# A prologue of attention: Wo's weights rounded earlier on ScalarE, five remainders made on GpSimd, and the first q lowered ahead of the first k

## The reference: what is computed

```
qkv = x @ Wqkv;  q, k, v = split(qkv)
q = rope(rmsnorm(q, q_norm_w));  k = rope(rmsnorm(k, k_norm_w))
mask = (i >= j) & (i - j <= 255)
probs = softmax(where(mask, q k^T / sqrt(32), -inf))
x = layernorm(x + (probs v) @ Wo)
shared = (silu(x @ Wg) * (x @ Wu)) @ Ws_down * sigmoid(x @ W_sgate)
x = layernorm(x + shared + sum over 2 experts of combine * expert(x))
```

## Time and profile before

| | |
|---|---|
| median of 3 runs | 1039.35 us (1038.63 to 1040.78) |
| the profiled execution | 1040.8 us, its span 1039.0 us |
| PE busy | 1016.2 us (98%) |
| DVE busy | 768.3 us (74%) |
| ACT busy | 639.3 us (62%) |
| POOL busy | 444.5 us (43%) |
| mean granted clock of TensorE | 0.996 of full speed |

### The profile page before, as it was taken

One profiled execution on the slowest core, in us unless ns is written; L12 is line 12 of the kernel. 1 busy time (PEld: TensorE's weight loads), 2 busy tenths in 40 slices (PEclk: granted clock), 3 DMA queues, 4 the chain that ended last, 5 costly groups with the idle time before them and its releaser, 6 DMA issues.

```text
span 1039.0 us, 19736 instructions
## 1 busy us (share of the span) xinstructions
PE 1016.2 (98%) x7088; PEld 838.1 (81%) x7088; DVE 768.3 (74%) x1163; ACT 639.3 (62%) x1310; POOL 444.5 (43%) x537
## 2 busy tenths in 40 slices
PE   7999999999999999999999999999999999999996
PEld 4677777777777777788888888888888888888884
DVE  6888877888888886596766777676677777667465
ACT  4666666666666765333766666666666666766344
POOL 2688888778888852000122222222222222221163
PEclk9999999999999999999999999999999999999999
DMA  5101111111111024735899999999999999999563
GB/s 194 55 23 44 33 33 33 37 51 34 33 44 33 22 84 147 238 91 167 248 260 264 262 272 266 268 264 256 258 281 259 263 266 271 256 249 255 130 209 146
DMA packets 120981, 171.36 MB, mean 165 GB/s; under 512 B 10114, under 2 KB 63746, under 8 KB 120804
## 3 DMA queue, kind: packets, MB, share of 16 engines
q1 hardware_dynamic: 111856, 149.54, 45.2%
q0 software_dynamic: 8736, 20.45, 11.9%
q10 hardware_dynamic: 292, 0.10, 0.0%
HBM read 151.45 MB, written 23.07 MB: 168 GB/s over the span
## 4 chain that ended last, share of the span: by engine, by line
PE 62%; DVE 1%; DMA 1%; ACT 1%; POOL 1%; issue 0%; SPq 0%; POOLq 0%; ACTq 0%; DVEq 0%
PE gate_ps L1614 4%; PE gate_ps L1616 4%; PE gate_ps L1615 4%; PE up_ps L1614 4%; PE up_ps L1616 4%; PE down_ps L1649 3%; PE up_ps L1615 3%; PE down_ps L1651 3%; PE down_ps L1650 3%; PE e_up_ps L1690 3%; PE e_up_ps L1692 3%; PE e_up_ps L1691 3%; PE e_gate_ps L1699 2%; PE e_gate_ps L1701 2%; PE e_gate_ps L1700 2%; PE e_up_ps L1701 2%
## 5 line engine op out<-in xcount | busy, mean ns | idle before, releaser
L1045 POOL DMA_INDIRECT sum_dram<-rows,target_i x39 | 67.0, 1718 | 358.1 <-ACT rows L1156 358.1
L1449 DVE TENSOR_TENSOR e_lo<-e_raw,e_hi 128x1408 fp32r<-128x1408 f32 x78 | 126.8, 1625 | 47.9 <-ACT e_hi L1130 47.8
L1130 ACT CAST e_hi<-e_raw 128x1408 fp32r<-128x1408 f32 x78 | 107.5, 1378 | 50.4 <-PE e_up_ps L1701 49.9
L337 ACT ACTIVATE prob<-score_ps,nbias 128x256 f32<-128x256 f32 (+1 forms) x256 | 118.2, 471 | 5.0 <-DVE nbias L466 5.0
L272 POOL TENSOR_TENSOR probT<-probT,masks 128x256 f32<-128x256 f32 x128 | 91.8, 745 | 55.4 <-DVE probT L496 55.4
L1454 DVE TENSOR_TENSOR ed_lo<-ed_raw,ed_hi 128x1024 fp32r<-128x1024 f32 x39 | 47.8, 1226 | 64.0 <-ACT ed_hi L1138 63.9
L466 DVE TENSOR_REDUCE nbias<-score_ps 128x2 f32<-128x512 f32 (+1 forms) x128 | 86.3, 675 | 4.4
L1051 POOL DMA_INDIRECT rows<-x_dram,token_i x39 | 50.2, 1287 | 88.7 <-DVE target_i L1416 65.1
L344 ACT COPY probT<-probT_ps 128x512 f32<-128x512 f32 x64 | 37.6, 587 | 78.9 <-PE probT_ps L612 78.8
L579 PE MATMUL proj_ps<-wqkv_lo,xT_hi 128*128 128x512 f32 x180 | 78.0, 434 | 1.2 <-ACT squares L358 1.2
L1614 PE MATMUL gate_ps<-x_hi,gu_lo 128*128 128x512 f32 x180 | 72.3, 402 | 0.6 <-DVE gu_lo L1304 0.6
(11 more groups left out here) (283 smaller groups left out, 2973.5 us busy)
## 6 DMA issues: line engine op xcount, KB each, us to landing
e_raw<-in_We_gu SPq DMA_DIRECT2D x78, 704.0 KB, 6.3
ed_raw<-in_We_down SPq DMA_DIRECT2D x39, 512.0 KB, 5.4
raw_ring<-in_Ws_gu SPq DMA_DIRECT2D x58, 256.0 KB, 6.4
wd_raw<-in_Ws_down SPq DMA_DIRECT2D x44, 256.0 KB, 6.5
gu_raw<-in_Ws_gu SPq DMA_DIRECT2D x30, 256.0 KB, 6.2
ed_raw<-in_We_down SPq DMA_DIRECT2D x39, 192.0 KB, 6.8
xT_in<-in_xT SPq DMA_DIRECT2D x16, 256.0 KB, 2.7
x_in<-in_x SPq DMA_DIRECT2D x16, 256.0 KB, 3.1
```

The costliest lines, as they stand in the source:

```text
L337: nc.scalar.activation(prob[:, g % 2, h, seen], score_ps[:, h, seen], ACT.Exp, bias=nbias[:, s % 2, head:head + 1], scale=1.0, accum_out=r ...
L1130: nc.scalar.copy(e_hi[:, half * HK:(half + 1) * HK, :], raw_half(i, half)).then_inc(e_hi_made, 1)
L1449: nc.vector.tensor_tensor(e_lo[:, part, :], raw_half(i, half), e_hi[:, part, :].bitcast(FP32), ALU.subtract).then_inc(e_lo_made, 1)
```

## The change

Three things change, all of them in the first 45 us.

- ScalarE rounds all four pieces of Wo one after the other in the prologue, behind `split_xT(1)` and ahead of `take_k(0)`, and no longer one in each group of block 0.
- GpSimd, behind the norms of the first q and k, makes the remainders of the values' second half (rows 2 and 3, 128x1024) and then those of Wo's four pieces (128x512 each); VectorE makes neither any more. They count on `cleared` (6, then 7 to 10), and TensorE waits for that.
- VectorE lowers the first q ahead of the first k.

```diff
--- before.py
+++ after.py
@@ -286,8 +286,16 @@
                     for keys in (kT_hi, kT_lo):
                         nc.gpsimd.tensor_copy(keys[:, :, a % RING, :], keys[:, :, key_slot(a % RING), :]).then_inc(kT_copied, 1)
 
+            def split_wo(k):
+                pool.wait_ge(w_hi_made, 6 + k + 1)
+                nc.gpsimd.tensor_tensor(wo_lo[:, k, :], wo_raw[:, k, :], wo_hi[:, k, :].bitcast(FP32), ALU.subtract).then_inc(cleared, 1)
+
             rms_of(0, 0, q_sq, q_var, q_rms)
             rms_of(0, 1, k_sq, k_var, k_rms)
+            pool.wait_ge(w_hi_made, 6)
+            nc.gpsimd.tensor_tensor(wqkv_lo[:, 2, 2:4, :], wqkv_raw[:, 2, 2:4, :], wqkv_hi[:, 2, 2:4, :].bitcast(FP32), ALU.subtract).then_inc(cleared, 1)
+            for k in range(KT):
+                split_wo(k)
 
             for s, g in steps():
                 a, n = s + 1, 4 * s + g - 1
@@ -398,13 +406,13 @@
             first_trig(1, k_rms, k_cs)
             take_q(0)
             split_xT(1)
+            for k in range(KT):
+                split_wo(k)
             take_k(0)
             take_v(0)
 
             for s, g in steps():
                 a, n = s + 1, 4 * s + g - 1
-                if s == 0:
-                    split_wo(g)
                 if g == 2 and has(s - 1):
                     wait(act, oT_made, s)
                     nc.scalar.copy(oT_hi[:, :, :], tiled(oT[:, :])).then_inc(oT_hi_made, 1)
@@ -445,10 +453,6 @@
                 dve.wait_ge(w_hi_made, 2 * c + i + 1)
                 nc.vector.tensor_tensor(wqkv_lo[part], wqkv_raw[part], wqkv_hi[part].bitcast(FP32), ALU.subtract).then_inc(w_lo_made, 1)
 
-            def split_wo(k):
-                dve.wait_ge(w_hi_made, 6 + k + 1)
-                nc.vector.tensor_tensor(wo_lo[:, k, :], wo_raw[:, k, :], wo_hi[:, k, :].bitcast(FP32), ALU.subtract).then_inc(w_lo_made, 1)
-
             def masked_max(s, g, pair):
 
                 done = 2 * (4 * s + g) + pair + 1
@@ -511,9 +515,8 @@
             dve.wait_ge(q_rot, 1)
             rotate_cos(dve, nc.vector, 0, 1, res[:, :], k_cs, k_weighted, k_part)
             rotate_sin(dve, nc.vector, 0, 1, res[:, :], oT[:, :], k_part, k_rot)
-            split_wqkv(2, 1)
+            lower_q(0)
             lower_k(0)
-            lower_q(0)
             split_xT(1)
             dve.wait_ge(masks_loaded, 16)
 
@@ -574,7 +575,9 @@
             def project(l_hi, l_lo, w_hi, w_lo, out, chunks, first=None):
 
                 for k in chunks:
-                    if first is not None:
+                    if first == 2 and k >= 2:
+                        pe.wait_ge(cleared, 6)
+                    elif first is not None:
                         pe.wait_ge(w_lo_made, 2 * first + k // 2 + 1)
                     nc.tensor.matmul(out, l_hi[:, k, :], w_lo[:, k, :], start=(k == 0), stop=False)
                     nc.tensor.matmul(out, l_hi[:, k, :], w_hi[:, k, :], start=False, stop=False)
@@ -696,7 +699,7 @@
                     wait(pe, v_made, min(a + 1, NB))
                     wait(pe, oT_lo_made, s)
                     if s == 1:
-                        wait(pe, w_lo_made, 6 + KT)
+                        wait(pe, cleared, 6 + KT)
                     part, done = (oT_hi, oT_lo, wo_hi, wo_lo, out_ps(s - 1)[:, 0, :]), wo_mm
                 between(s, g)
                 if part:
```

## The result

Measured: **1045.05 us** (median of 6 runs, 1044.25 to 1045.99), against 1038.91 for the kernel before on the same chips; ratio 1.0057, 95% interval 1.0047 to 1.0067, 6.1 us slower. Forecast were 1044.7 and +5.3: 0.35 us off in the time and 0.8 off in the change, as the median of before is 0.44 lower here than the 1039.35 that the forecast started from. The profiled execution took 1045.47 us.

A forecast was written before the change was run, and what follows sets the result against it. TensorE, busy 98% of the span, bounds the kernel, so only its waits in the first 45 us count. Later first scores give +5.3, all else 0: 1039.35 + 5.3 = 1044.7 us; overall range 1040.7 to 1046.8.

The forecast's parts named there:

- Part 1: Prologue, ScalarE: Wo's four early casts fit ahead of k's rounding and cost nothing, bounds 0 and 0.
- Part 2: Prologue: GpSimd's remainders take turns with VectorE's k rotation, which ends at 27.01 in place of 21.60, 5.4 us later.
- Part 3: TensorE after k's rotation: transposes and values' second half at the lower clock, first scores 30.4 for 25.1, +5.3 us.
- one microsecond more if the lower level outlasts the scores: TensorE behind the first scores: a possible 1 us more from the lower clock, not counted in the sum.
- the stretch from the first scores to 1020 as long as before: Sign for the profile after: from first scores to 1020 us, no change in length.
- Part 4: VectorE, q ahead of k and one values' remainder gone: brings nothing with k late; 0.46 gain were k not late.
- Part 5: Block 0 without Wo's casts and remainders: gain taken as 0, bounded by TensorE's 2.41 us idle there.
- 1 fell: k's rotation: only the values' remainder gets between, Wo's don't; +1.4 to +2.2, 1040.8 to 1041.5; chance 0.11.
- 2 fell: k's rotation: GpSimd work really hidden, not slower; 1038.9, down to 1036.5; chance 0.09.
- 3 fell: GpSimd in the prologue: subtraction into fp32r slow by itself, 2.14 per 128x512; scores +9.7, 1049.0; chance 0.08.

The follow-up runs named there:

- e_spare_write: Kernel before plus 14 zero fills of 128x512 on GpSimd, which only write SBUF, beside k's rotation; 1038.53 us against 1038.93 before, ratio 0.9999.
- e_order: Kernel before with the first q lowered ahead of the first k, nothing else; 1038.81 us against 1038.93 before, ratio 0.9998.
- e_spare_read: Kernel before plus six more GpSimd subtractions of 128x512, reading SBUF, where the change has its five remainders; 1045.75 us against 1038.93 before, ratio 1.0073.
- e_all_late: Changed kernel with one more wait: GpSimd's five remainders start only at the end of k's rotation; 1040.70 us against 1038.93 before, ratio 1.0022.
- e_fill: Changed kernel plus 12 matmuls of no use in TensorE's idle time ahead of k's transposes; 1043.14 us against 1039.13 before, ratio 1.0042.
- e_wo_late: Changed kernel with the values' remainder back on VectorE and GpSimd's Wo remainders held until k's rotation ends; 1039.15 us against 1039.13 before, ratio 1.0004.

## Why the prediction was right, step by step

- **Part 1, the early casts**: nothing, as forecast. They run from 19.66 to 21.84, and ScalarE's next work, k's rounding, starts at 27.92.
- **Part 2, the turns**: right to 0.15 us. The rotation's end was forecast 5.4 later, and was 26.70 + 0.16 = 26.86 on before's time axis for 21.60, +5.3. Each instruction came out as its own length less 0.14 behind the other engine's, to 0.04. The rule of the Trainium skill ("SBUF — State Buffer", "Who interferes with whom") holds here as it was cited, for reads; e_spare_write shows its other half, that GpSimd instructions which only write don't block.
- **Part 3**: first scores forecast 5.3 later; A grew by 5.4. The choice of the lower level for all of it was right: transposes at 26.76 and scores at 30.37 are 3.6 apart, 3.3 forecast; most of the rest lies in the first of the six matmuls (0.58 to the next one and not 0.43) and behind the last (0.56 to the scores).
- **What was undersized** is the term that the working named and put at nothing, "one microsecond more if the lower level outlasts the scores": it did, by 2.3 us of time, and B grew by 0.98. 5.43 + 0.98 = 6.4 in the profiled runs, 6.1 in the medians, and so the sign "the stretch from the first scores to 1020 as long as before" failed by that 1 us. That 1044.7 lies within 0.35 of the measured time is in part luck: the change was 0.8 larger than forecast, and the median of before came out 0.44 lower. The terms named for the upper end of the range give 1039.35 + 6.3 + 1 = 1046.65, not 1046.8.
- **Part 4**: nothing, as forecast; k's late rotation covers it. In the kernel before the swap is worth at most what e_order shows, nothing that can be told.
- **Part 5**: nothing, as forecast. The first instruction of the next q's rotation (L193) starts at 38.14 and takes 1.07, held by GpSimd's mask product, where it took 0.68 before: it ends 6.25 later than before, near the 6.4 of the first scores of block 1.
- **Rivals.** 1 fell (L201, L202 and L204 each gave a turn), 2 fell (the four lengths, and e_spare_read), 3 fell: Wo's four remainders take 5.49 us, 1.37 each, in e_all_late, with the wait for one instruction of VectorE in it, the tokens' remainder (1.59 there).
- Open: when the lower clock comes and goes within the prologue. It was there from about 20.1 to 23.5 in the profiled run of before, and not at all in e_order's, whose program is the same up to the end of k's rotation; what decides it was not tried.

## What to carry to other kernels

Before work is moved to an engine with room, look at what it reads and when: here each GpSimd subtraction that read SBUF cost VectorE nearly its whole duration (1.06 of 1.30 us at L201) at a two-operand SBUF instruction that it met, and a queue of several took a turn between each two. It has to start where VectorE reads PSUM or has slack, and its queue has to be through before its engine's next due work; both limits showed here, 5 us of A (e_all_late) and 1 us of B. And the stall of TensorE was paid twice here, in its own length and in the clock behind it (about 1.9 us, e_fill).

## What was not expected of the hardware

The lower clock level in the prologue is not fixed in place from run to run. TensorE idles 1.64 and then 1.01 us ahead of the first half of the values in the profiled run of before, and 1.65 and 1.01 in e_wo_late's, and the granted clock from 15 to 35 us is 0.91 and 0.83: the lower level lasts from 20.1 to 23.5 in the one and from 17.7 to 24.5 in the other. In e_order's, at 1.00 throughout, the first of the two gaps is shorter, 1.32: there the lower level at k's projection lasted until 14.5 (matmuls 0.43 apart until then) and not until 13.2, so TensorE was through later. Whether that difference decides is not shown. The level moves A by up to 1.6 us (5.97 in e_order to 7.54 in e_wo_late, which have the same order ahead of the first scores and no delay in the rotation), so that a gain of half a microsecond at this place can be read in neither a single profile nor these medians.
